# A selective-scan stage: C's broadcast loads by blocks of 32 partitions, B's loads issued by ScalarE

## What is computed

```python
xs = jnp.stack([s0, s1, s0[..., ::-1], s1[..., ::-1]], axis=1)      # K = 4 orders
dts, Bs, Cs = jnp.split(x_dbl, [DT_RANK, DT_RANK + D_STATE], axis=2) # 16 rows of B, 16 of C
delta = jax.nn.softplus(dts + dt_projs_bias[None, :, :, None])
def step(hst, inp):
    u_t, d_t, B_t, C_t = inp
    hst = hst * jnp.exp(d_t[..., None] * A) + (d_t * u_t)[..., None] * B_t[:, :, None, :]
    return (hst, jnp.einsum('bkdn,bkn->bkd', hst, C_t))
```

## Time and profile before

| | us |
|---|---|
| median of 3 executions | 11659.61 |
| lowest, highest | 11655.64, 11695.09 |
| the profiled execution | 11717.54 |
| its span, first to last instruction | 11715.7 |

### The profile page before, as it was taken

How to read it: one execution, slowest core, us unless ns; L and a number is a source line. 1 busy time by engine, 2 the same in 40 slices (tenths; PEclk the granted TensorE clock), 3 DMA queues, 4 the chain that set the end, 5 groups by cost and what they waited for, 6 DMA issues and landing times. The chain is left out here.

```text
span 11715.7 us, 504765 instructions
## 1 busy us (share of the span) xinstructions
PE 9928.2 (85%) x225056; PEld 5034.1 (43%) x225056; DVE 8362.1 (71%) x7894; ACT 7093.5 (61%) x13093; POOL 8419.5 (72%) x4027
## 2 busy tenths in 40 slices
PE   7888888888888888888888888888888888888886
PEld 3444344443444434444344443444434444344443
DVE  4888658876578856888568885688756887568885
ACT  4666546665566655666556664566645666456664
POOL 3888548886488854888458884588845888458884
PEclk9999899998999989999899998999988999899997
DMA  3555225552255523555135551355513555145551
GB/s 89 139 136 142 68 71 137 142 137 66 74 137 141 139 61 87 137 142 142 45 91 141 141 136 43 98 140 137 134 44 97 137 141 136 42 106 136 142 140 30
DMA packets 1609070, 1301.68 MB, mean 111 GB/s; under 512 B 1272943, under 2 KB 1274512, under 8 KB 1540860
## 3 DMA queue, kind: packets, MB, share of 16 engines
q1 hardware_dynamic: 1606908, 1269.37, 41.2%
HBM read 832.67 MB, written 33.55 MB: 74 GB/s over the span
## 5 line engine op out<-in xcount | busy, mean ns | idle before, releaser
L1376 DVE TENSOR_TENSOR_SCAN arena<-arena,ps 128x512 f32<-128x512 f32 x6144 | 7339.1, 1254 | 1883.8 <-issue 842.2
L475 POOL TENSOR_TENSOR arena<-arena 128x1024 f32<-128x1024 f32 x3072 | 7204.2, 2368 | 1362.0 <-ACT arena L646 744.5
L664 ACT ACTIVATE arena<-arena,negA 128x512 f32<-128x512 f32 x6144 | 4056.2, 711 | 1987.3 <-DMA arena<-arena 1359.6
L1007 PE MATMUL ps<-arena 64*32 64x128 f32 x196608 | 3938.1, 281 | 936.3 <-issue 574.4
L1007 PEld LDWEIGHTS ps<-arena 64*32 64x32 f32 x196608 | 2927.1, 108 | 3341.3 <-issue 3327.0
L1046 PE MATMUL ps<-arena,gather 128*32 128x512 f32 x12288 | 2195.4, 634 | 59.1 <-POOL arena L475 46.1
L646 ACT ACTIVATE arena<-arena 128x2 f32<-128x2 f32 x2688 | 527.4, 196 | 918.1 <-DVE arena L1376 909.3
L939 PE MATMUL ps<-arena,wconv 96*64 96x512 f32 (+1 forms) x2304 | 827.8, 624 | 23.7 <-issue 23.7
L459 POOL TENSOR_TENSOR arena<-arena,u_hi 128x512 f32<-128x512 f32 x256 | 325.7, 1272 | 684.4 <-ACT arena L606 684.4
L1046 PEld LDWEIGHTS ps<-arena,gather 128*32 128x32 f32 x12288 | 368.1, 111 | 679.9 <-issue 584.4
L964 PE MATMUL ps<-u_lo,xw_lo 128*128 128x512 f32 x1024 | 586.5, 656 | 55.4 <-SPq L165 47.2
(11 more groups left out here) (164 smaller groups left out, 6431.6 us busy)
## 6 DMA issues: line engine op xcount, KB each, us to landing
arena<-b_runs SPq DMA_DIRECT2D x512, 1024.0 KB, 7.0
arena<-arena SPq DMA_DIRECT2D x6144, 64.0 KB
arena<-c_rows SPq DMA_DIRECT2D x512, 512.0 KB
arena<-in_x SPq DMA_DIRECT2D x128, 192.0 KB, 2.7
out_tokens<-arena SPq DMA_DIRECT2D x64, 192.0 KB, 2.4
c_rows<-arena SPq DMA_DIRECT2D x256, 32.0 KB
b_runs<-arena SPq DMA_DIRECT2D x512, 16.0 KB
b_runs<-arena SPq DMA_DIRECT2D x4, 1024.0 KB, 9.2
```

What stands on the lines that cost most here:

```text
L475: pool.tensor_tensor(h, h, c_rep[s // NG], ALU.mult).then_inc(weighted, 1)
L664: act.activation(hst[s][:, a, :], delta_rep[:, g, :], ACT.Exp, scale=negA[:, ch.k, i:i + 1]).then_inc(decay_ready, 1)
L1007: mm = pe.matmul(to, du_t[ch.par][rows, k, g * CW:(g + 1) * CW], spots[rows, j, :], start=True, stop=True)
L1376: dve.tensor_tensor_scan(hst[s][:, a, :][:, flip], hst[s][:, a, :][:, flip], drive(s % 2)[:, :, a][:, flip], before, ALU.mult, ALU.add).th ...
```

## The change

C's load becomes four transfers, one for each block of 32 partitions, each reading one row of 4 KB 32 times; the semaphore's counts are four times as high (NJ = 4). B's two loads leave SP's queue: ScalarE issues them, in its own DMA queue, with the waits that SP had, at steps 7 and 11 of the chunk before, between its save of the state and the decays of that step. In the prologue of an image ScalarE issues both after `save_bt` and before `save_du`.

```diff
-                            wait_apart(sp, c_loaded[pr], ch.n(16, -16))
+                            wait_apart(sp, c_loaded[pr], ch.n(16 * NJ, -16 * NJ))
...
-                    def load_b(pr):
-                        if not ch.first:
-                            wait_apart(sp, drive_ready, ch.n(NSTEP, (pr + 1) * NG - NSTEP))
-                        wait_apart(sp, b_written, ch.n(16 * 2, 16 * 2))
-                        rows = f_dram[par].rearrange("(p w) -> p w", w=TROW)[:, pr * NB * PITCH:(pr + 1) * NB * PITCH]
-                        sp.dma_start(b_diag[pr].rearrange("p k w -> p (k w)"), rows).then_inc(b_loaded[pr], 16)
-
                     def load_c(pr):
                         if not ch.first:
                             wait_apart(sp, weighted, ch.n(NSTEP, (pr + 1) * NG - NSTEP))
                         wait_apart(sp, c_written, ch.n(16, 16))
-                        rows = c_dram[par][pr * RUN:(pr + 1) * RUN, :]
-                        sp.dma_start(c_rep[pr], rows.rearrange("(j a) t -> j (a t)", a=2).unsqueeze(1).to_broadcast([NJ, CW, 2 * T])).then_inc(c_loaded[pr], 16)
+                        rows = c_dram[par][pr * RUN:(pr + 1) * RUN, :].rearrange("(j a) t -> j (a t)", a=2)
+                        for j in range(NJ):
+                            sp.dma_start(c_rep[pr][j * CW:(j + 1) * CW, :], rows[j:j + 1, :].to_broadcast([CW, 2 * T])).then_inc(c_loaded[pr], 16)
...
                     load_delta(2)
-                    load_b(0)
                     load_delta(0)
                     load_c(0)
                     load_delta(1)
-                    load_b(1)
                     load_c(1)
...
-                            pool.wait_ge(c_loaded[s // NG], ch.n(16, 16))
+                            pool.wait_ge(c_loaded[s // NG], ch.n(16 * NJ, 16 * NJ))
...
+                def load_b(ch, pr):
+
+                    if not ch.first:
+                        act.wait_ge(drive_ready, ch.n(NSTEP, (pr + 1) * NG - NSTEP))
+                    act.wait_ge(b_written, ch.n(16 * 2, 16 * 2))
+                    rows = f_dram[ch.par].rearrange("(p w) -> p w", w=TROW)[:, pr * NB * PITCH:(pr + 1) * NB * PITCH]
+                    act.dma_start(b_diag[pr].rearrange("p k w -> p (k w)"), rows).then_inc(b_loaded[pr], 16)
+
...
                     save_bt(ch)
+                    load_b(ch, 0)
+                    load_b(ch, 1)
                     save_du(ch, 0)
...
+                            if s == 7:
+                                load_b(nx, 0)
+                            if s == 11:
+                                load_b(nx, 1)
                             if s == 9:
                                 save_du(nx, 0)
```

## The result

The changed kernel is slower: 11749.48 us (10 executions, 11711.82 to 11787.29) beside 11684.49 us for the kernel before (10 executions, 11617.49 to 11700.05). The ratio is 1.0069, 95% interval 1.0051 to 1.0086. The forecast was 11445 us in a range of 11270 to 11650, so the time moved the other way.

A forecast was written before the change was run, and what follows sets the result against it. A closed loop through ACT and SP's delta loads, 34.73 us a chunk, sets the pace. +1.85 - 2.28 - 0.65 = -1.08 us, taken as -0.8 x 248 = -198, with image starts -214, gave 11445 us, range 11270 to 11650.

The forecast's parts named there:

- The loop: ACT's steps 4 to 7, SP's delta issues and the landing tail close a cycle of 34.73 us, one chunk.
- C0's three issues: On SP's queue, C0 in four blocks adds three issues, +1.85 us in the cycle.
- B0 leaving SP: Taking B0's issue out of SP's queue shortens the cycle by 0.65 us.
- ACT's wait and issue at step 7: On ACT, B0 waits 0.8 us and issues in 0.44; step 10's exponentials start 1.2 late, absorbed by idle time.
- C's blocks: C no longer holds four engines, so the tail after load_delta(1) falls from 4.94 to 2.66 us, saving 2.28.
- B1 should start 1 us after load_delta(1)'s first issue and be through before its last.: Argument against the slower rival: B1's stream from ACT's queue would not delay the end of load_delta(1).
- The slower rival: B1 in ACT's queue takes its share beside load_delta(1); cycle 1.2 us longer, +298 us, 11957 us; chance 0.10.
- break-even tail of 3.74: Tail after load_delta(1)'s issues at which the change gains nothing (4.94 + 0.65 - 1.85); above it, the forecast is wrong.
- C's blocks bring nothing: C's blocks don't spread or take as long; tail stays 4.94, three issues are paid, 11957 us; chance 0.03.
- PE binds at once: PE's issue waits grow and absorb the gain: 0 to 0.2 us a chunk, 11610 to 11660 us; chance 0.14.
- Its waits for ACT: Sign in the profile after: PE's waits for ACT, 31.9 us in the window, would be halved.
- What is late next is PE with DVE: PE's own loop is about 1.1 us shorter than a chunk, so 0.2 to 0.3 of the 1.08 is given back.

The follow-up runs named there:

- e11: Kernel before with C's load in blocks of 32 partitions alone, B's loads left on SP, a second run: 11563.71 us, ratio 0.9844.
- e8: Changed kernel with B1 alone issued by SP again, behind load_delta(1), B0 still on ACT: 11505.46 us, ratio 0.9905 to the kernel before.
- e9: Kernel before with C in one transfer over 16 engines and B0 issued by ACT, B1 on SP: 11378.50 us, ratio 0.9691.
- e12: Kernel before with C's rows written four times to DRAM, each C load one transfer over 16 engines, second run: 11420.82 us, ratio 0.9733.
- e7: Kernel before, unchanged, run again for a trace on the same chip: 11622.01 us, a single execution.
- a2: Changed kernel run again, unaltered, on the same chip as other runs: 11763.05 us, ratio 1.0126 to the kernel before.
- e1: Kernel before with C's load in blocks of 32 partitions alone, B's loads left on SP, first run: 11639.00 us, ratio 0.978.
- e4: Kernel before with C's rows written four times to DRAM, each C load one transfer over 16 engines, first run: 11530.77 us, ratio 0.9694.
- e2: Kernel before with only B0 and B1 moved to ACT's queue, C one transfer on four engines: 12600.21 us, ratio 1.0588.

## Why the prediction was wrong, step by step

**The loop was right.** It is the cycle ACT, SP, tail that sets the pace: its terms sum to the chunk before (34.73 in the one worked out) and after. The chunk worked out had a shorter tail, 4.44, than the mean of 4.72; the 4.94 that was taken is near it. **C0's three issues** were right (+1.84 for +1.85), and so, taken alone, was **B0 leaving SP** (-0.80 for -0.65). **ACT's wait and issue at step 7** cost next to nothing, as forecast (0.3 us of wait a chunk, 0.33 us an issue; ACT's stretch of the cycle is 0.11 longer). **C's blocks** do what was argued: with B left in SP's queue the tail falls by 2.47 us (e11), a little more than 2.28, and the chunk by 0.31 (34.74 for 35.05, on different chips).

**What failed, first: "B1 should start 1 us after load_delta(1)'s first issue and be through before its last."** In the chunk shown B1 was issued 1.68 us after the first (611.19 - 609.51) and its rows ran from 612.17 to 616.45, past the last issue (615.01). On average the forecast timing was nearly met: the rows start 0.5 us after the first issue and end 0.3 us after the last one's start. But B1's place hangs on ACT and load_delta(1)'s on SP, so the two shift against each other, and in 143 of 239 chunks the stream ends after the last issue has started. Where it ends before, the tail is 3.12 us, near e8's 2.91; where it ends late, 3.94 and 4.77. A single time for a stream that moves was the error: the early chunks gain nothing to pay for the late ones. The tail fell by 1.51 instead of 2.28, 0.77 short. e8 shows the cause by taking B1 alone away: the tail is 2.91 for 3.93, and the chunk 1.01 us shorter. The slower rival had this mechanism. It was priced as B1 taking a share, with a break-even tail of 3.74 (from the end of the issues). Measured from there, the tail is 3.91 - 0.81 = 3.1 us (the last issue takes 0.81), so by this term alone the kernel would still have been a little faster.

**Second: "B0 leaves SP: -0.65 in the cycle", with the issues of load_delta(0) left as they were.** They take 0.73 us more. It is one pattern over all runs: first to last issue 4.74 to 4.85 us in the seven profiled executions with B0 on SP, 5.43 to 5.52 in the seven with B0 on ACT; e9 and e12 differ in B0 alone and have 5.49 and 4.81. The third to sixth of the eight issues take 0.78 to 0.89 us in the kernel after, 0.60 to 0.63 before. With +0.73 the gain of 0.80 by moving B0 is gone: from load_delta(2)'s first issue to load_delta(0)'s last it is 11.73 us for 11.80.

That moving B0 does this is shown, by what means is not. It isn't that B0's rows move beside these issues, for they did so before too: from 0.45 to 4.95 us after the first issue in e7, and from 1.6 us ahead of it to 3.1 us behind it in a2. Nor does every stream from ACT's queue do it: load_delta(1)'s issues take 5.22 us beside B1 in the kernel after, and 5.29 in e8, where B1 comes behind them. What else has changed is that sixteen issues of delta now follow each other on SP with nothing between. No run keeps these apart.

The whole miss, from -1.08 to +0.56, is 1.64 us a chunk: 0.77 for the tail, 0.73 for load_delta(0)'s issues, 0.19 for load_delta(1)'s, 0.11 for ACT, less 0.15 for B0 and 0.01 for C0. The 0.19 comes with C's blocks (e11 has 5.30 us with B on SP), not with B1. No step of the forecast allowed delta's own issues to become longer.

**The rivals.** *Slower, B1 beside load_delta(1)*, at 0.10, named the first of the two failed steps; the second it didn't have, and its 11957 us was 208 too much. That the time fell on its side is in part luck: without load_delta(0)'s 0.73 us the cycle would be 0.17 us shorter than before, by the table. *C's blocks bring nothing* falls with the tails of e1 and e11. The rule of the Trainium skill behind it ("DMA: Bandwidth & Descriptors", "Rules for kernel authors") presumes transfers that spread over all 16 engines, and the whole C transfer had four. *PE binds at once* falls too. What PE waited for in the kernel after, 230 to 1250 us:

```profile
PE ps L1013 <- issue: 58.3, 43, 4.4
...
PE ps L986 <- ACT arena L607: 20.6, 8, 4.1
PE ps L1036 <- ACT y_hi L655: 12.8, 11, 2.4
```

PE's issue waits are 58.3 us for 62.9. Its waits for ACT didn't halve (20.6 + 12.8 = 33.4 for 31.9), since ACT's step 4 comes no earlier. "What is late next is PE with DVE" was right, as e12 shows: below some 34.2 us a chunk ACT waits for PE and DVE.

**Not settled.** The kernel before took 11684, 11905, 11608 and 11733 us in the four comparisons, and 11905 and 11608 came from the same chip. What moves it by 2.6% was not found. Ratios of one group stand beside the same kernel before; but where it was slow (e1 to e4) they may flatter, so the terms of the loop and differences inside a group carry more than a ratio of 1 or 2%. Within the stream of B1 PE's fills often stop where the profile shows no releaser (the longest gap inside step 2's fill is 1.5 us on average for 0.6 before); over a whole chunk these stops don't add up to more, and whether they cost anything where they fall was not tried apart. Nor was it found by what means B0's move lengthens load_delta(0)'s issues.

## What to carry to other kernels

A bulk transfer in a second DMA queue doesn't wait its turn behind small transfers on which the loop depends: here it stopped them for close to 3 us at a time. Put it in the same queue behind them, or start it where its whole stream falls clear of them in every round of the loop and not only in the one looked at; a queue's fixed order is also a priority. When a transfer is slow, look at its DMA share first: one with a slowest dimension of 4 used four engines, and copies in DRAM that bring the dimension to 16 gave the gain of splitting it without the issues (e4 and e12). And sum the closed loop term by term after the change as well: here it showed which terms had given back the gain.

## What the runs showed of the hardware

**Two queues do not share evenly in time.** Two stretches of the kernel after (length, busy engines, clock, DMA share, GB/s):

```profile
230.00:1250.00 1020.00, 888.61 (x24456) 470.09 (x24461) 819.20 (x687) 671.21 (x1285) 873.83 (x402) 0.95 0.53 137
612.00:615.00 3.00, 2.89 (x116) 1.68 (x116) 3.00 (x4) 2.34 (x5) 3.00 (x3) 1.00 1.00 300
```

While B1 streams in this chunk all 16 engines are full (share 1.00), and delta stands for 2.87 us; of B1's 128 rows each engine has 8, if they are spread evenly, at 340 to 370 ns each once it runs, 2.7 to 3.0 us. That is what one would see if an engine finished its eight rows of B before it went back to the other queue.
The Trainium skill, page "DMA: Bandwidth & Descriptors", section "Queues, rings and completion order", says that an engine goes round its queue rows and drains a whole packet of descriptors, typically 9 to 17, from one before it switches. By that, the trace agrees: eight rows are no more than one packet.
The Trainium skill, same page, section "Issuing engines are not separate DMA queues", says that issuing from several engines saves only the time of issuing. Here that was 0.80 us a chunk, of which 0.07 were left once load_delta(0)'s issues had become longer, and the rest was a loss: +5.9% in e2, where C held four engines as well.

**An issue's duration isn't fixed.** The same eight issues on SP took 4.74 us with B0 issued by SP ahead of them, and 5.47 us with B0 issued by ACT. The issue of B took 0.33 us on ACT, where on SP its median was 0.44.
